# GNN kernel, second layer: the q of a group is picked and spread at the head of a step

## The reference

```python
h = jnp.maximum(_layernorm(x), 0.0)                     # layer 0: 16 relation types
x = x + segment_sum(sum_r (h[src] * (etype == r)) @ weight[r], dst)
h = jnp.maximum(_layernorm(x), 0.0)                     # layer 1: an MLP per edge
msg = relu(concat([h[src], h[dst], edge_attr]) @ W1 + b1) @ W2 + b2
x = x + segment_sum(msg, dst)
```

## Time and profile before

| | |
|---|---|
| median of 3 runs | 4229.12 us (4224.97 to 4232.71) |
| profiled execution, first to last instruction | 5160.7 us |
| mean granted clock of TensorE, share of full speed | 0.681 |
| GpSimd busy in the profiled execution | 3161.4 us (61%) |
| TensorE matmul busy | 2728.2 us (53%) |
| DVE busy | 1473.2 us (29%) |
| ScalarE busy | 582.7 us (11%) |

### The profile page before, as it was taken

How to read it: one execution, slowest core, us unless ns; L and a number is a source line. 1 busy time by engine, 2 the same in 40 slices (tenths; PEclk the granted TensorE clock), 3 DMA queues, 4 the chain that set the end, 5 groups by cost and what they waited for, 6 DMA issues and landing times.

```text
span 5160.7 us, 36581 instructions
## 1 busy us (share of the span) xinstructions
PE 2728.2 (53%) x10312; PEld 1524.6 (30%) x10312; DVE 1473.2 (29%) x2000; ACT 582.7 (11%) x1138; POOL 3161.4 (61%) x3350
## 2 busy tenths in 40 slices
PE   2655555555555555455555455554454554554555
PEld 1433333333333333333332222222222222222222
DVE  6322222222222222222233233233232333232232
ACT  3111111111111111111110000010000010000010
POOL 7466565566666566656646566665665666665665
PEclk9776677776767667676766666666666666666666
DMA  4111111111111111111111111111111111111111
GB/s 95 21 24 23 23 26 23 23 26 24 24 25 24 23 24 26 24 23 25 24 27 30 27 29 28 30 30 26 31 29 26 31 30 28 29 29 26 31 29 26
DMA packets 392815, 144.34 MB, mean 28 GB/s; under 512 B 323186, under 2 KB 338859, under 8 KB 392795
## 3 DMA queue, kind: packets, MB, share of 16 engines
q0 software_dynamic: 106496, 109.26, 11.1%
q1 hardware_dynamic: 283685, 34.22, 4.6%
q10 hardware_dynamic: 2614, 0.62, 0.1%
HBM read 129.23 MB, written 12.83 MB: 28 GB/s over the span
## 4 chain that ended last, share of the span: by engine, by line
another core or an unknown queue 33%; PE 24%; issue 21%; POOL 9%; DVE 7%; DVEq 1%; DMA 1%; ACT 1%; SPq 1%; POOLq 0%; ACTq 0%
POOL rows L711 9%; PE ps L1333 7%; PE ps L1407 5%; PE ps L1406 4%; PE ps L1411 2%; DVE q_blk L1211 2%; DVE z_slot L1198 2%; PE ps L1347 2%; PE ps L1340 1%; DVE slots L1187 1%; DVEq L1202 1%; DMA rows<-h_table,idx 1%; PE ps L1306 1%; PE ps L1307 1%
## 5 line engine op out<-in xcount | busy, mean ns | idle before, releaser
L711 POOL DMA_INDIRECT rows<-p_table,idx x1664 | 1574.4, 946 | 959.7 <-issue 527.3
L711 POOL DMA_INDIRECT rows<-h_table,idx x1616 | 1528.2, 946 | 999.0 <-issue 461.4
L1406 PE MATMUL ps<-w_attr,attr_t 64*128 64x512 f32 x416 | 363.2, 968 | 1156.8 <-DVE q_blk L1211 873.1
L1333 PE MATMUL ps<-onehot,rows 128*64 128x256 f32 x3328 | 704.9, 555 | 455.1 <-DMA rows<-h_table,idx 371.2
L1060 DVE TENSOR_TENSOR onehot<-key,ps 128x2048 f32<-128x2048 f32 x209 | 474.1, 2276 | 556.6 <-remote 439.7
L1333 PEld LDWEIGHTS ps<-onehot,rows 128*64 128x64 f32 x3328 | 355.4, 196 | 728.5 <-issue 663.4
L1340 PE MATMUL ps<-w_types,slots 128*128 128x128 f32 x3328 | 455.5, 294 | 96.3 <-issue 78.5
L1340 PEld LDWEIGHTS ps<-w_types,slots 128*128 128x128 f32 x3328 | 424.4, 207 | 151.9 <-issue 131.0
L1187 DVE TENSOR_TENSOR slots<-ps,rows 128x512 f32<-128x512 f32 x208 | 143.9, 692 | 1052.9 <-remote 438.9
L1406 PEld LDWEIGHTS ps<-w_attr,attr_t 64*128 64x128 f32 x416 | 85.9, 256 | 1195.7 <-issue 1195.7
L1407 PE MATMUL ps<-q_blk,onehot 128*128 128x512 f32 x416 | 411.0, 1090 | 0.0
(11 more groups left out here) (136 smaller groups left out, 1693.0 us busy)
## 6 DMA issues: line engine op xcount, KB each, us to landing
rows<-p_table,idx POOLq DMA_INDIRECT x1664
rows<-h_table,idx POOLq DMA_INDIRECT x1616
attr<-in_edge_attr_dram SPq DMA_DIRECT2D x52, 128.0 KB
q_win<-q_table SPq DMA_DIRECT2D x208, 32.0 KB
p_table<-pq_out SPq DMA_DIRECT2D x25, 120.0 KB
q_table<-pq_out SPq DMA_DIRECT2D x25, 120.0 KB
out_dram<-xs SPq DMA_DIRECT2D x25, 120.0 KB
xs<-in_x_dram SPq DMA_DIRECT2D x6, 480.0 KB, 6.5
```

The source lines that it names most:

```text
L711: pool.indirect_dma_start(rows[:, u, t, :], None, table, bass.IndirectOffsetOnAxis(ap=idx[:, u, t:t + 1], axis=0)).then_inc(s, 16)
L1333: last = pe.matmul(slot_ps[t % 2 * D:(t % 2 + 1) * D, b, t // 2, :], rows[:, u, t, :], onehot[:, b, t, :], start=True, stop=True)
L1406: pe.matmul(pre_ps[:, u % 2, :], attr_t[half, u // 2, :], w_attr[half].rearrange("k j d -> k (j d)"), start=True, stop=False)
```

## The change

In the steps with u % 4 not 0, TensorE's `pick_q(u)` and DVE's `spread_q(u)` go to the head of the step, ahead of the products and the addition of the group before. In the steps with u % 4 = 0 they follow directly on these. The wait for the spread, which stood in `products`, now stands in the step, for the group before: there q_blk and q_ps are both guarded by it. After the loop one wait for all 208 spreads is added.

```diff
                 def step(it, u, first=False):            # DVE
+                    if u % B:
+                        spread_q(it, u)
                     if not first or u >= 1:
                         add_rows(*back(it, u, 1))
+                    if u % B == 0:
+                        spread_q(it, u)
...
                         reduce_z(*back(it, u, 2))
-                    spread_q(it, u)
...
                 def products(it, u):                     # TensorE
-                    wait_apart(pe, q_spread, it * U + u + 1)
...
                 def step(it, u, first=False):
+                    if u % B:
+                        wait_apart(pe, q_spread, it * U + u)
+                        pick_q(it, u)
                     if not first or u >= 1:
+                        if u % B == 0:
+                            wait_apart(pe, q_spread, it * U + u)
                         products(*back(it, u, 1))
+                    if u % B == 0:
+                        pick_q(it, u)
                     if not first or u >= 3:
                         place_z(*back(it, u, 3))
                     if not first or u >= 2:
                         sum_group(*back(it, u, 2))
-                    pick_q(it, u)
...
+                wait_apart(pe, q_spread, G)
                 products(NIT - 1, U - 1)
```

## The result

| kernel | median, us | lowest to highest, us | runs | ratio with 95% interval |
|---|---|---|---|---|
| before | 4229.41 | 4224.97 to 4232.71 | 4 | |
| changed | 4272.39 | 4261.66 to 4273.49 | 4 | 1.0093 [1.0081, 1.0106] |

The changed kernel takes 43.0 us more. The forecast was 4227 us in a range of 4182 to 4242, with a chance of 0.07 for slower: the time lies outside the range and on the other side.

What follows compares the result with a forecast made beforehand. It took timed runs to be bound by GpSimd's gathers, 9.99 us a group, with hardly a wait left. Parts (a), (c) and (d) came to 0, with at most 9 us to win; it said 2 us: 4229 - 2 = 4227, range 4182 to 4242.

Steps and rivals of the forecast that it cites:

- (c): Second layer's loop: gathers need 9.99 us a group, above loops of 8.1 and 6.2 us, so the shorter loop gains 0.
- I take the late releases to be a cost of the tracing: TensorE's late releases after bursts of short instructions exist only under the trace, so removing such waits gains nothing when timed.
- the sum of waits: GpSimd's waits before gathers in both layers, 940.3 us, set against the 931.6 us between profiled span and timed median.
- a timed run that is bound by the gathers: Whole kernel untraced: gathers with hardly a wait left, 4220.4 us without waits, at most 9 us left to win.
- (a): TensorE: the pick moves to the head in six steps of eight, costing 0.53 us in either place, so 0.
- (b): DVE: the 0.68 us spread leaves the tail, products run beside mask to reduce; loop from about 8.1 to 6.2 us.
- (d): First steps and tail: the last addition waits for the last rows as before, with the same chain behind it, 0.
- the late window: Slower rival: pick waits for its window load in steps 2 and 6, 52 x 1 us, 4281 us; chance 0.06.
- The prediction's two signs of being wrong: A timed median under 4200 us, or a pick starting late behind its window transfer with the addition behind it.
- The first rival: GpSimd's waits before two groups a turn are real untraced: 3.5 us less each, 182 us, 4047 us; chance 0.09.
- The forecast's own sign for this case: Under the trace, GpSimd's waits for L1187 drop from 432 us by about 100 to 180 and the span falls.

Runs made afterwards that it cites:

- e1_swap: The kernel before with only the one-hots put ahead of the spread in DVE's tail: 4264.61 us against 4222.32 for before.
- e3_pe_alone: The kernel before with only TensorE's half of the change, picks at the head of the step, DVE in its old order: 4222.29 us against 4222.32.
- e17: The same kernel, TensorE's half of the change alone on the kernel before, run again: 4222.99 us against 4222.62.
- e9: The changed kernel with the one-hots' number row read from PSUM and the W2 product moved from step 6 to 7: 4222.09 us against 4222.68 for before.
- e13_double: The changed kernel plus a spare comparison with two SBUF inputs in the other two steps of four, long session: 5049.19 us against 5198.77 for before.

## Why the prediction was wrong

**The step that failed** is (c), "the gathers need 9.99 us a group" and with it "GpSimd's distance of 9.99 us a group stays". I took the length of a gather as given, because everything that waited for it had time to spare, and asked of each moved instruction only who waits for it. A gather also depends on what DVE does while it starts. The part on DVE costed the spread that moves, and not what the spread leaves behind: the one-hots come 0.6 us earlier, though no edit touches them. Term (c) had 0; it measured +42.3 us in e1_swap. The rows were to be had. In the trace of before 19 gathers of the second layer take over 1.0 us, and each of them has a one-hot beside it. One of them stands 5 us behind the addition of 3564.42 in the earlier trace rows:

```profile
3569.20 0.69 DVE L1211 TENSOR_TENSOR q_blk<-ps,blocks 128x512 f32<-128x512 f32 x1 [0.84 <-issue]
3569.80 0.68 DVE L1171 TENSOR_TENSOR onehot<-key,iota_f 128x512 f32<-128x512 f32 x1
3569.99 1.31 POOL L711 DMA_INDIRECT rows<-p_table,idx  x1 [0.30 <-issue]
```

1.31 us among rows of 0.94 asks for a reason, and its neighbour names it: 104 one-hots at 0.37 us would have been a rival at +38 us, decided by where the one-hot starts against the gather. The Trainium skill (SBUF — State Buffer, Who interferes with whom) has the rule: a DVE instruction with two inputs in SBUF contends with a GpSimd instruction that reads SBUF, one with a single SBUF input doesn't, and who issues first blocks the other. The runs agree with the first two: a gather, which reads its indices from SBUF, takes 0.94 to 0.96 us behind a spread or one-hot with one SBUF input and 1.00 to 1.54 us behind one with two. Of the third they show one side: where the gather is first it takes its 0.94 us, but the one-hot behind it takes its 0.68 us too, so no run shows DVE blocked for the length of a gather. The same section says that a probe saw no DMA stalled by such an instruction, and infers that writing the descriptors isn't in its way. Here an indirect DMA was held; whether it was its reading of indices or its writing of descriptors no run shows.

**"I take the late releases to be a cost of the tracing"** failed as well. The sum of waits, 940.3 us, did account for the difference between profile and timed runs, and the profiles of short sessions have hardly any waits for DVE (none in the changed kernel), so "a timed run that is bound by the gathers" was right. The reason was not. A profile of 4222.7 us (e3_pe_alone) is traced too, timed runs take 5200 us in long sessions, and behind the same burst a short session's trace shows no late release. So neither the sum of waits nor the bursts spoke for the tracing. It did not move the number, but the profile was taken for false when it was a true one of another condition.

**What held.** (a) TensorE's half is worth 0 (e3, e17). (b) The loop is shorter: by the recorded ends, a group's products end 10.5 us (median) ahead of its addition in the changed kernel, and 2.7 us ahead in e1_swap, which has pick and spread in their old places. Both are ahead, so, as the prediction said, this is worth nothing in a short session. (d) Nothing at the ends: e3 and e9 are level with before as wholes. The pick does not wait for its window: of TensorE's 511.8 us of idle time ahead of it in the changed kernel 318.6 us end with DVE's spread and 193.2 us with ScalarE's copy of the one-hots, and windows land in 1.8 us. So the slower rival, the late window, had the right sign and not its mechanism. The prediction's two signs of being wrong, a median under 4200 us and a pick that starts late behind its window, did not come; it failed by a path that none of its rivals had.

**The first rival**, waits that are real, is what a long session shows: 182 us worked out, 141.8 measured for the changed kernel. Its mechanism, the spread that no longer stands between the products' release and the next addition, fits the longest wait, 4.2 us shorter; that the missing 40 us are the held gathers is spoken against by e13_double, which has more of them and gained 149.6 us. The forecast's own sign for this case, waits for L1187 that drop by 100 to 180 us and a profiled span that falls, is there: 126.5 us, and 5093.6 us against 5177.9.

## What to carry to other kernels

Before an instruction is moved, write down what slides into its place, and compare it with what the bounding engine starts at that moment: for GpSimd's indirect DMAs, a DVE instruction with both inputs in SBUF (seen here with a comparison and with the layer norm's scalar_tensor_tensor). Where two engines run in step a collision of 0.4 us isn't chance but comes back every turn, so a mean that rises by 24 ns is worth a look at the single rows. And when the profile's own time and the timed runs lie 20% apart, have the two measured together before a number is built on either.

## What the runs showed of the hardware

A DVE comparison of 128x512 with two SBUF inputs (0.68 us) held an indirect DMA on GpSimd from about 0.12 us after the DMA's start to DVE's own end. In the 18 traces with such comparisons in the second layer, all 959 that start 0.03 to 0.49 us ahead of a gather held it, and it took 1.01 to 1.47 us instead of 0.94. Of the 1018 that start 0.05 us or more behind the nearest gather's start none held it. Between the two lies the border: of 109 there 88 held the gather, which then took up to 1.54 us. Comparisons of the same size with one input in PSUM, spreads with one input in PSUM, and reduces with one input held nothing at the same place.

A whole kernel of 4222 us took 5132 to 5273 us in some sessions, two of its chips having given 4222 us in others. Its gathers took the same 0.95 us. The time lies in waits of GpSimd, in both layers, for work that waits for TensorE's results. What sets it off stays open.
